# Retrieval scores: the mean's place among the splits, an earlier chunk load, and the groups in which three gathered sums are turned

## The chip, the cores and the metric

One core of one Trainium2 chip runs the whole kernel in one launch. The metric is the device time of a launch in microseconds (us). TensorE (PE), VectorE (DVE), ScalarE (ACT), GpSimd (POOL) and the issue queue of SyncE (SP) run their own instruction streams and meet only at semaphores.

## The reference

Sizes: B = 512 rows, K = 50 indices for each, a table of V = 12500 items of H = 512 numbers, all float32.

```python
retrieved = jnp.mean(item_embeddings[indices], axis=1)
fused_input = jnp.concatenate([user_rep, retrieved], axis=1)
fused_rep = fused_input @ W_fuse + b_fuse
logits = fused_rep @ W_proj + b_proj
```

Many indices lie beyond the table and stand for its last row, so the rows to be fetched are fewer than 50 for each output row.

## The kernel before

**Tiles, chunks, groups.** The 512 rows are four tiles of 128. The 12500 columns of the output are 25 chunks of 500. A group is one tile times one chunk: 12 matmuls of 500 columns, since each product is taken in three parts (the weights and the fused rows are both split into a rounded part, `w_hi` and `f_hi`, and a remainder, `w_lo` and `f_lo`). The groups of tile 0 have one matmul more, for the bias. Chunks 0 to 7 stay in SBUF ("resident"): the kernel runs tile 0 over its eight groups, then tiles 1, 2 and 3. Chunks 8 to 24 are then streamed, each for all four tiles.

**A chunk of weights.** SP loads it in two halves into `w_raw` (two chunks deep, L186); ACT writes `w_hi` (`split_hi`, L316, one instruction a half), DVE writes `w_lo` (`split_lo`, L478, likewise). The load of chunk c waits until the `w_lo` of chunk c - 2 is written. Tile 0's group c waits for both `w_lo` halves of chunk c.

**The gathered sum of a tile.** DVE first sorts the tile's indices (`sort`), so that those inside the table come first. POOL then issues 17 gathers of one row for each partition (L256), each into one slot of a ring of nine, plus gathers into `home` for what is beyond (one, and a second after the copy of L285). A gather waits until the one nine before it has been summed. Columns past a row's last index are skipped inside the gather, so the late gathers of a tile move little. In tile 0, DVE sums the first nine slots and TensorE the other eight and `home` (L582), which leaves the sum turned in a PSUM bank. In tiles 1 to 3 DVE sums all 17 (`add`, L450, `add_pair` for two), `add_last` (L464) and `add_home` (L473); the seventeenth add writes `total`, and TensorE turns it with four transposes (`turn_sum`, L590).

**From the sum to the groups.** ACT scales the turned sum into `ret_t` (`mean`, L328); TensorE multiplies it with the second half of W_fuse (`fuse`, L599, 32 matmuls); ACT writes `f_hi` (`fused_hi`, L333), DVE `f_lo` (`fused_lo`, L491). Tile t + 1 is turned in the middle of tile t's seventh group (c = 6) and fused right behind that group, for all t.

**Banks and stores.** The resident groups and the turned sums of tiles 1 to 3 take three PSUM banks in turn, so each waits for the evacuation of the one three places before. ACT evacuates tile 0's groups (`evacuate_first`, L340), DVE all others (`evacuate`, L506, adds the bias). `out_sb` has three slots; an evacuation waits for the store three groups before it.

**Order on SP ahead of the groups.** After the first loads: wait for tile 0's slot 16, the last of its gathers, then loads of chunks 2 to 5, then for c = 0 and 1 the load of chunk c + 6, a row of the bias, the store of tile 0's group c, and so on. ACT's order there is `split_hi(2)`, `split_hi(3)`, `mean(0)`, `fused_hi(0)`; DVE's is `bias_lo`, `sort(3)`, `add_last(1)`, adds 0 and 1 of tile 1, `split_lo(2)`, adds 2 and 3, `split_lo(3)`, add 4, `fused_lo(0)`.

Of the kernel before, what the change touches and what calls it, by code (L numbers as in the profile page):

```python
# [23 lines left out]
LAPS_AT = 12  # L24
DVE_FIRST = 9
PE_FIRST = PASSING - DVE_FIRST
AHEAD = 5
TURN_EVERY = RESIDENT + 1
HOME_AFTER = 14
OUT_SLOTS = 3  # L30
BIAS_SLOTS = 8
# [3 lines left out]
def retrieval_scores(nc, user_t_in, indices, table, w_fuse, b_fuse, last_item, w_proj, b_proj, out):  # L35
# [4 lines left out]
    LAST = V - 1  # L40
    COLUMNS = SORTED + K
    assert B == TILES * P and H == HK * P and V % CHUNK == 0 and (CHUNKS - 1) % RESIDENT == 0
    assert BASE < SORTED < K and AHEAD + 2 * (RESIDENT - 2) == PASSING
# [7 lines left out]
    with ExitStack() as ctx:  # L51
# [102 lines left out]
        def place(t, i):  # L154
            return (PASSING * t + i) % RING
# [4 lines left out]
        def adds_done(t, i):  # L160
            return (DVE_FIRST + PASSING * (t - 1) if t else 0) + i + 1

        def turn_bank(t):
            return wide_ps[(TURN_EVERY * t - 2) % 3] if t else first_ps

        def group_bank(t, c):
            return wide_ps[(TURN_EVERY * t + c + (c == RESIDENT - 1 and t + 1 < TILES)) % 3]

        def group_of(t, c):
            return TILES * c + t if c >= RESIDENT else RESIDENT * t + c  # L170
# [9 lines left out]
        @block.sync  # L180
        def _(sp):
            def load_chunk(c):
                for h in range(2):
                    if c >= 2:
                        sp.wait_ge(lo_ready, 2 * (c - 2) + h + 1)
                    sp.dma_start(w_raw[:, c % 2, 2 * h:2 * h + 2, :],  # L186
                                 wp_dram[:, 2 * h:2 * h + 2, c * CHUNK:(c + 1) * CHUNK])\
                      .then_inc(w_landed[c % 2][h], 16)

            def load_bias(c):  # L190
                sp.dma_start(bias[:, c % BIAS_SLOTS:c % BIAS_SLOTS + 1, 0:CHUNK],
                             bp_dram[:, c * CHUNK:(c + 1) * CHUNK].unsqueeze(1).to_broadcast([P, 1, CHUNK]))\
                  .then_inc(bias_landed[c % BIAS_SLOTS], 16)

            def store(t, c):
                g = group_of(t, c)
                wait_evacuated(sp, g)
                sp.dma_start(out_dram[t, :, c * CHUNK:(c + 1) * CHUNK], out_sb[:, g % OUT_SLOTS, :])\
                  .then_inc(out_stored[g % OUT_SLOTS], 16)

            sp.dma_start(idx[:, 0:K], indices[:, 0:K]).then_inc(first_idx_landed, 16)
            for k in range(HK):
                sp.dma_start(wf_user[:, k, :], wf_dram[0, :, k, :]).then_inc(wf_user_landed[k], 16)
                if k == 0:
                    sp.dma_start(idx[:, K:TILES * K], indices[:, K:TILES * K]).then_inc(idx_landed, 16)
            sp.dma_start(last_rows[:], last_item.to_broadcast([P, H])).then_inc(last_landed, 16)
            load_chunk(0)
            sp.dma_start(bf_col[:], b_fuse).then_inc(bf_landed, 16)
            load_chunk(1)
            sp.dma_start(wf_ret[:], wf_dram[1]).then_inc(wf_ret_landed, 16)  # L210
            sp.wait_ge(user_fused, 1)
            for row in (0, LO_ROW):
                sp.dma_start(bias_rows[row:row + RESIDENT, :],
                             b_proj[0:RESIDENT * CHUNK].rearrange("(c n) -> c n", n=CHUNK))\
                  .then_inc(bias_rows_landed, 16)
            sp.wait_ge(slot_landed[place(0, PASSING - 1)], 16 * slot_uses(0, PASSING - 1))
            for c in range(2, 6):
                load_chunk(c)
            for c in range(RESIDENT):
                if c < 2:  # L220
                    load_chunk(c + 6)
                if c < RESIDENT - 1:
                    load_bias(c)
                store(0, c)
            load_bias(RESIDENT - 1)
            for c in range(RESIDENT):
                store(1, c)
                if c < 2:
                    load_chunk(RESIDENT + c)
            for c in range(RESIDENT):  # L230
                store(2, c)
            for c in range(RESIDENT):
                store(3, c)
                load_bias(RESIDENT + c)
                if c in (3, 5):
                    load_chunk(RESIDENT + 2 + c // 4)
            for c in range(RESIDENT, CHUNKS):
                for t in range(TILES):
                    store(t, c)
                if c + BIAS_SLOTS < CHUNKS:  # L240
# [65 lines left out]
        def _(act):  # L306
# [45 lines left out]
            act.wait_ge(bias_rows_landed, 32)  # L352
            nc.scalar.copy(bias_split, bias_rows).then_inc(bias_hi_ready, 1)
            split_hi(2)
            split_hi(3)
            mean(0)
            act.wait_ge(bf_landed, 16)
            fused_hi(0)
            for c in range(RESIDENT):
                if c < 2:  # L360
                    split_hi(c + 4)
                if c == RESIDENT - 2:
                    mean(1)
                if c == RESIDENT - 1:
# [11 lines left out]
        def _(dve):  # L376
# [156 lines left out]
            dve.wait_ge(laps_ready, 1)  # L533
            add_home(0)
            bias_lo()
            sort(3)
            add_last(1)
            add_pair(1, 0)
            split_lo(2)
            add_pair(1, 2)  # L540
            split_lo(3)
            add(1, 4)
            fused_lo(0)
            for t in range(TILES):
                for c in range(RESIDENT):
                    if t + 1 < TILES and c < RESIDENT - 2:
                        add_pair(t + 1, AHEAD + 2 * c)
                        if AHEAD + 2 * c + 1 == HOME_AFTER:
                            add_home(t + 1)
                    if t == 0 and c < 4:  # L550
                        split_lo(c + 4)
                    if t + 2 < TILES and c >= RESIDENT - 2:
                        if c == RESIDENT - 2:
                            add_last(t + 2)
                        add_pair(t + 2, 2 * (c - RESIDENT + 2))
                    if t == TILES - 1 and 2 <= c < 6:
                        split_lo(RESIDENT + c // 2 - 1, (c % 2,))
                    if c == RESIDENT - 1 and t + 1 < TILES:
                        fused_lo(t + 1)
                    if t:  # L560
                        evacuate(t, c)
                if t + 2 < TILES:
                    add(t + 2, 4)
            for c in range(RESIDENT, CHUNKS):
                for t in range(TILES):
                    evacuate(t, c)
# [4 lines left out]
        def _(pe):  # L571
# [13 lines left out]

            def turn_sum(t):
                pe.wait_ge(added, adds_done(t, PASSING - 1))
                wait_evacuated(pe, group_of(t - 1, RESIDENT - 4))
# [27 lines left out]
            def project_resident(t, c, halfway=None):  # L616
                g = group_of(t, c)
                if t == 0:
                    pe.wait_ge(lo_ready, 2 * (c + 1))
                if c == RESIDENT - 1 and t + 1 < TILES or t and c == 0:  # L620
                    wait_evacuated(pe, g - 2)
                elif g >= 3:
                    wait_evacuated(pe, g - 3)
# [34 lines left out]
            fuse(0)  # L658
            for t in range(TILES):
                for c in range(RESIDENT):  # L660
                    halfway = t + 1 if c == RESIDENT - 2 and t + 1 < TILES else None
                    project_resident(t, c, halfway)
                    if halfway is not None:
                        fuse(halfway)
# [41 lines left out]
```

## Time and profile before

| what | value |
|---|---|
| runs | 348.36, 352.34, 346.40 us; median 348.36 |
| profiled execution | 348.81 us, of which the span is 347.0 |
| TensorE busy | 322.1 us (93% of the span) |
| DVE, POOL, ACT busy | 183.1, 83.4, 67.5 us |
| granted TensorE clock, mean | 0.97 |
| HBM | 55.47 MB read, 25.60 MB written |

The profile is of one execution. "Idle before" is the time an engine stood still ahead of an instruction; what ended it is inferred from semaphores. Starts are given from the beginning of the span, and 1.8 us of the execution lie outside it.

### The profile page before, as it was taken

What the parts mean: (1) busy time and instruction counts of PE and PEld (TensorE: products, weight loads), DVE (VectorE), ACT (ScalarE), POOL (GpSimd) and SP (SyncE); (2) the same over time, 40 slices, a digit from 0 to 9 for tenths busy, and PEclk for the clock granted to TensorE, in tenths of its full rate; (3) what the DMA queues carried; (4) which work ended last, traced back from release to release, by engine and by line L of the source; (5) the groups of instructions that cost most, each with busy time, mean ns of one, the idle gap of its engine ahead of it and who ended that gap; (6) DMA issues with size and microseconds to landing.
All of it is one profiled execution on the core that took longest, in us unless ns stands there. A gap on an engine that the chain in (4) does not pass through costs nothing.

```text
span 347.0 us, 4203 instructions
## 1 busy us (share of the span) xinstructions
PE 322.1 (93%) x1462; PEld 263.9 (76%) x1462; DVE 183.1 (53%) x294; ACT 67.5 (19%) x102; POOL 83.4 (24%) x87
## 2 busy tenths in 40 slices
PE   4987269969999999999999999999999999999996
PEld 2447268859888888888888888888888888888884
DVE  5698459784667872453454344543445434454222
ACT  2320326522002002403122022220222220220000
POOL 4777777657675700000000000000000000000000
PEclk9998769978999999999999999999999999999999
DMA  7992997996897521589478766787667665452222
GB/s 265 375 361 50 373 401 193 361 379 187 236 389 258 146 107 41 151 225 353 141 226 241 200 165 234 223 240 198 170 231 226 209 228 170 149 188 91 112 94 89
DMA packets 40238, 75.24 MB, mean 217 GB/s; under 512 B 5686, under 2 KB 34630, under 8 KB 40224
## 3 DMA queue, kind: packets, MB, share of 16 engines
q1 hardware_dynamic: 33312, 60.11, 53.1%
q0 software_dynamic: 6336, 13.92, 12.2%
q10 hardware_dynamic: 576, 1.05, 0.8%
q8 instruction: 6, 0.10, 0.1%
q14 instruction: 8, 0.07, 0.1%
HBM read 55.47 MB, written 25.60 MB: 234 GB/s over the span
## 4 chain that ended last, share of the span: by engine, by line
PE 79%; DMA 8%; issue 4%; DVE 4%; POOL 3%; ACT 1%; SPq 0%; POOLq 0%; DVEq 0%; ACTq 0%
PE bank L612 73%; DMA w_raw<-w_proj 5%; PE bank L599 5%; POOL ring L256 3%; DMA ring<-item_embeddings,rows 2%; DVE bank L450 2%; DMA out_sb<-indices 1%; DVE w_lo L478 1%; ACT w_hi L316 1%; PE bank L590 1%; SPq L186 0%; DVE f_lo L491 0%; DVE total L450 0%; DVE bank L473 0%; DVE out_sb L506 0%
## 5 line engine op out<-in xcount | busy, mean ns | idle before, releaser
L612 PE MATMUL bank<-w_hi,f_hi 128*128 (+1 forms) x400 | 156.5, 391 | 0.0
L612 PE MATMUL bank<-w_lo,f_hi 128*128 (+1 forms) x400 | 155.8, 389 | 0.0
L612 PE MATMUL bank<-w_hi,f_lo 128*128 (+1 forms) x400 | 155.5, 389 | 0.0
L506 DVE TENSOR_TENSOR out_sb<-bank,early 128x500 f32<-128x500 f32 x92 | 62.4, 678 | 130.5 <-PE bank L612 125.8
L612 PEld LDWEIGHTS bank<-w_hi,f_lo 128*128 128x128 f32 x400 | 75.4, 188 | 15.6
L612 PEld LDWEIGHTS bank<-w_hi,f_hi 128*128 128x128 f32 x400 | 75.5, 189 | 15.5 <-DVE f_lo L491 0.3
L612 PEld LDWEIGHTS bank<-w_lo,f_hi 128*128 128x128 f32 x400 | 75.5, 189 | 15.0
L316 ACT CAST w_hi<-w_raw 128x1000 fp32r<-128x1000 f32 x50 | 51.0, 1030 | 164.3 <-DMA w_raw<-w_proj 145.9
L256 POOL DMA_INDIRECT ring<-item_embeddings,rows x68 | 70.6, 1038 | 32.0 <-issue 18.2
L478 DVE TENSOR_TENSOR w_lo<-w_raw,w_hi 128x1000 fp32r<-128x1000 f32 x50 | 59.2, 1194 | 2.4 <-ACT w_hi L316 2.4
L450 DVE SCALAR_TENSOR_TENSOR bank<-ring,mask,bank 128x512 f32<-128x512 f32 x56 | 42.3, 755 | 9.7 <-DMA ring<-item_embeddings,rows 6.9
L599 PE MATMUL bank<-ret_t,wf_ret 128*128 128x128 f32 x128 | 17.8, 306 | 9.9 <-ACT ret_t L328 9.9
L599 PEld LDWEIGHTS bank<-ret_t,wf_ret 128*128 128x128 f32 x128 | 17.8, 223 | 10.4 <-issue 10.1
L576 PE MATMUL bank<-early 128*128 128x512 f32 x32 | 16.3, 667 | 4.9 <-DMA early<-w_fuse 4.9
L576 PEld LDWEIGHTS bank<-early 128*128 128x128 f32 x32 | 6.7, 216 | 13.0 <-issue 13.0
L328 ACT ACTIVATE ret_t<-bank 128x128 f32<-128x128 f32 x16 | 3.1, 281 | 41.7 <-PE bank L590 41.7
L491 DVE SCALAR_TENSOR_TENSOR f_lo<-bank,bf_col,f_hi 128x128 fp32r<-128x128 f32 x16 | 4.5, 345 | 10.2 <-ACT f_hi L333 10.2
L582 PE MATMUL bank<-ret_t,ring 128*128 128x128 f32 x32 | 5.4, 322 | 3.8 <-DMA ring<-item_embeddings,rows 3.7
L256 POOL DMA_INDIRECT home<-item_embeddings,lap_row x4 | 7.4, 1844 | 3.6 <-POOL lap_row L285 2.5
L582 PEld LDWEIGHTS bank<-ret_t,ring 128*128 128x128 f32 x32 | 4.7, 225 | 4.3 <-issue 4.3
L333 ACT ACTIVATE f_hi<-bank,bf_col 128x128 fp32r<-128x128 f32 x16 | 4.6, 369 | 14.9 <-PE bank L599 14.9
L340 ACT COPY out_sb<-bank 128x500 f32<-128x500 f32 x8 | 4.6, 576 | 10.4 <-PE bank L612 7.9
(58 smaller groups left out, 55.1 us busy)
## 6 DMA issues: line engine op xcount, KB each, us to landing
w_raw<-w_proj SPq DMA_DIRECT2D x50, 500.0 KB, 6.6
logits<-out_sb SPq DMA_DIRECT2D x100, 250.0 KB, 2.4
early<-b_proj SPq DMA_DIRECT2D x25, 250.0 KB, 5.2
ring<-item_embeddings,rows POOLq DMA_INDIRECT x68, 5.8
early<-user_t ACTq DMA_DIRECT2D x4, 256.0 KB, 4.4
early<-w_fuse SPq DMA_DIRECT2D x4, 256.0 KB, 6.0
wf_ret<-w_fuse SPq DMA_DIRECT2D x1, 1024.0 KB, 18.5
last_rows<-last_item SPq DMA_DIRECT2D x1, 256.0 KB, 7.0
```

The lines of the kernel that those rows point to most:

```text
L256: return nc.gpsimd.indirect_dma_start(out=to, out_offset=None, in_=table, in_offset=bass.IndirectOffsetOnAxis(ap=column, axis=0), **how)
L316: nc.scalar.copy(w_hi[:, slot, 2 * h:2 * h + 2, :], w_raw[:, c % 2, 2 * h:2 * h + 2, :])\
L333: nc.scalar.activation(f_hi[:, t, n, :], fused_ps[n][:, t * P:(t + 1) * P], ACT.Identity, bias=bf_col[:, n:n + 1]).then_inc(f_hi_ready, 1)
L340: nc.scalar.copy(out_sb[:, c % OUT_SLOTS, :], group_bank(0, c)[:, 0:CHUNK]).then_inc(first_evacuated, 1)
L450: nc.vector.scalar_tensor_tensor(total[:] if i == PASSING - 1 else total_ps[:], here, mask[:, t, i + 1:i + 2], total_ps[:], ALU.mult, ALU. ...
L478: nc.vector.tensor_tensor(w_lo[:, c % RESIDENT, 2 * h:2 * h + 2, :], w_raw[:, c % 2, 2 * h:2 * h + 2, :], w_hi[:, c % RESIDENT, 2 * h:2 * ...
L491: nc.vector.scalar_tensor_tensor(f_lo[:, t, n, :], fused_ps[n][:, t * P:(t + 1) * P], bf_col[:, n:n + 1], f_hi[:, t, n, :].bitcast(F32), A ...
L506: nc.vector.tensor_tensor(out_sb[:, g % OUT_SLOTS, :], ps[:, 0:CHUNK], bias[:, c % BIAS_SLOTS, 0:CHUNK], ALU.add).then_inc(evacuated, 1)
L576: m = nc.tensor.matmul(fused_ps[n][:, :], wf_user[:, k, n * P:(n + 1) * P], user_t[:, k, :], start=(k == 0), stop=(k == HK - 1))
L582: m = nc.tensor.matmul(first_ps[:, k * P:(k + 1) * P], rows_in[:, k * P:(k + 1) * P], taken, start=(first and k == 0), stop=last, skip_gro ...
L599: m = nc.tensor.matmul(fused_ps[n][:, t * P:(t + 1) * P], wf_ret[:, k, n * P:(n + 1) * P], ret_t[:, k, :], start=False, stop=(k == HK - 1) ...
L612: m = nc.tensor.matmul(ps[:, 0:CHUNK].unsqueeze(1), f[:, t, k, :], w, start=begin, stop=(f is f_lo and k == HK - 1))
```

## The change

ACT takes `mean(0)` between `split_hi(2)` and `split_hi(3)`. SP loads chunk 2 behind a wait for slot 12 of tile 0, and chunks 3 to 5 behind the old wait for slot 16. DVE does `split_lo(2)` ahead of `sort(3)`, and has its adds of tile 1 placed later, behind `split_lo(3)` and `fused_lo(0)`, still five of them ahead of the loop. A table, `TURN_AT = (6, 5, 5)`, says in which group of tile t the next tile is turned: tile 1 still in the seventh, tiles 2 and 3 now in the sixth. The adds of a tile are dealt out to the groups by that table, `split_lo(7)` moves from the fourth group of tile 0 to its seventh, and the order of the banks is read from a list (`bank_order`) with its waits (`bank_freed`).

```diff
-AHEAD = 5
-TURN_EVERY = RESIDENT + 1
+TURN_AT = (6, 5, 5)
...
+        bank_order = []
+        for t in range(TILES):
+            for c in range(RESIDENT):
+                bank_order.append((t, c))
+                if t + 1 < TILES and c == TURN_AT[t]:
+                    bank_order.append((t + 1, "turn"))
+
         def turn_bank(t):
-            return wide_ps[(TURN_EVERY * t - 2) % 3] if t else first_ps
+            return wide_ps[bank_order.index((t, "turn")) % 3] if t else first_ps
...
+        def bank_freed(engine, t, c):
+            place_before = bank_order.index((t, c)) - 3
+            if place_before >= 0 and bank_order[place_before][1] != "turn":
+                wait_evacuated(engine, group_of(*bank_order[place_before]))
...
+            sp.wait_ge(slot_landed[place(0, LAPS_AT)], 16 * slot_uses(0, LAPS_AT))
+            load_chunk(2)
             sp.wait_ge(slot_landed[place(0, PASSING - 1)], 16 * slot_uses(0, PASSING - 1))
-            for c in range(2, 6):
+            for c in range(3, 6):
                 load_chunk(c)
...
             split_hi(2)
+            mean(0)
             split_hi(3)
-            mean(0)
             act.wait_ge(bf_landed, 16)
             fused_hi(0)
...
             bias_lo()
+            split_lo(2)
             sort(3)
             add_last(1)
-            add_pair(1, 0)
-            split_lo(2)
-            add_pair(1, 2)
+            add(1, 0)
             split_lo(3)
-            add(1, 4)
+            add(1, 1)
             fused_lo(0)
+            add(1, 2)
+            add_pair(1, 3)
             for t in range(TILES):
+                turn_at = TURN_AT[t] if t + 1 < TILES else RESIDENT
+                ahead = PASSING - 2 * turn_at
                 for c in range(RESIDENT):
-                    if t + 1 < TILES and c < RESIDENT - 2:
-                        add_pair(t + 1, AHEAD + 2 * c)
-                        if AHEAD + 2 * c + 1 == HOME_AFTER:
+                    if c == RESIDENT - 1 and t + 1 < TILES:
+                        fused_lo(t + 1)
+                    if t + 1 < TILES and c < turn_at:
+                        add_pair(t + 1, ahead + 2 * c)
+                        if ahead + 2 * c + 1 == HOME_AFTER:
                             add_home(t + 1)
-                    if t == 0 and c < 4:
-                        split_lo(c + 4)
-                    if t + 2 < TILES and c >= RESIDENT - 2:
-                        if c == RESIDENT - 2:
+                    if t == 0 and c in (0, 1, 2, RESIDENT - 2):
+                        split_lo(min(c + 4, RESIDENT - 1))
+                    if t + 2 < TILES and c >= turn_at:
+                        if c == turn_at:
                             add_last(t + 2)
-                        add_pair(t + 2, 2 * (c - RESIDENT + 2))
+                        add_pair(t + 2, 2 * (c - turn_at))
...
-                if t + 2 < TILES:
-                    add(t + 2, 4)
+                for i in range(2 * (RESIDENT - turn_at), PASSING - 2 * TURN_AT[t + 1] if t + 2 < TILES else 0):
+                    add(t + 2, i)
...
                 for c in range(RESIDENT):
-                    halfway = t + 1 if c == RESIDENT - 2 and t + 1 < TILES else None
+                    halfway = t + 1 if t + 1 < TILES and c == TURN_AT[t] else None
                     project_resident(t, c, halfway)
```

## Rows read from the trace of the kernel before

**Rows 1.** TensorE's idle times: waiting line, releaser, us in total, times, longest

```profile
PE bank L599 <- ACT ret_t L328: 9.9, 1, 9.9
PE bank L590 <- DVE total L450: 3.2, 1, 3.2
```

**Rows 2.** The chain that ended last: start us, us, what

```profile
46.66 4.74 PE bank L599 x26
...
74.72 1.11 PE bank L590 x4
...
78.34 4.76 PE bank L599 x32
...
103.72 0.44 PE bank L590 x4
...
105.51 3.57 PE bank L599 x32
```

**Rows 3.** Timeline of ACT: start us, us, instructions [idle before]

```profile
45.31 1.02 ACT L316 CAST w_hi<-w_raw 128x1000 fp32r<-128x1000 f32 x1 [1.86 <-DMA w_raw<-w_proj]
46.24 0.77 ACT L328 ACTIVATE ret_t<-bank 128x128 f32<-128x128 f32 x4
```

**Rows 4.** POOL's gathers for tile 0 (12, 16), tile 1 (16), tile 2 (16)

```profile
25.92 1.34 POOL L256 DMA_INDIRECT ring<-item_embeddings,rows  x1 [0.30 <-issue]
...
31.48 0.99 POOL L256 DMA_INDIRECT ring<-item_embeddings,rows  x1 [0.30 <-issue]
...
58.26 0.99 POOL L256 DMA_INDIRECT ring<-item_embeddings,rows  x1 [0.39 <-issue]
...
91.16 1.01 POOL L256 DMA_INDIRECT ring<-item_embeddings,rows  x1 [1.24 <-DVE bank L450]
```

**Rows 5.** DMA issues one by one, us to landing: gathers at 25.92, 31.48, 58.26

```profile
ring<-item_embeddings,rows POOLq DMA_INDIRECT x1, 3.5
ring<-item_embeddings,rows POOLq DMA_INDIRECT x1, 2.1
ring<-item_embeddings,rows POOLq DMA_INDIRECT x1, 6.3
```

**Rows 6.** The same of SP: chunk 2's halves (33.59, 34.03), a store at 61.6

```profile
w_raw<-w_proj SPq DMA_DIRECT2D x1, 500.0 KB, 4.2
w_raw<-w_proj SPq DMA_DIRECT2D x1, 500.0 KB, 5.7
logits<-out_sb SPq DMA_DIRECT2D x1, 250.0 KB, 8.2
```

**Rows 7.** Timeline of TensorE: the last sum of tile 0

```profile
35.68 1.06 PE L582 MATMUL bank<-out_sb,ring 128*128 128x128 f32 x8
```

**Rows 8.** Timeline of DVE: sort(3) begins, add_last(1), fused_lo(0), loop, totals of tiles 1, 2

```profile
31.48 0.21 DVE L394 MAX8 key_sorted<-out_sb 128x8 f32<-128x50 f32 x1
...
33.70 0.76 DVE L464 TENSOR_SCALAR bank<-last_rows,n_left 128x512 f32<-128x512 f32 x1 [0.20 <-DVE rows L406]
...
51.88 1.13 DVE L491 SCALAR_TENSOR_TENSOR f_lo<-bank,bf_col,f_hi 128x128 fp32r<-128x128 f32 x4 [3.64 <-ACT f_hi L333]
52.92 1.61 DVE L450 SCALAR_TENSOR_TENSOR bank<-ring,mask,bank 128x512 f32<-128x512 f32 x2
...
56.73 1.60 DVE L450 SCALAR_TENSOR_TENSOR bank<-ring,mask,bank 128x512 f32<-128x512 f32 x2
...
73.92 0.75 DVE L450 SCALAR_TENSOR_TENSOR total<-ring,mask,bank 128x512 f32<-128x512 f32 x1
...
101.31 0.75 DVE L450 SCALAR_TENSOR_TENSOR total<-ring,mask,bank 128x512 f32<-128x512 f32 x1
```

**Rows 9.** Stretches: PE busy, PEld, DVE, ACT, POOL, granted clock, DMA share, GB/s

```profile
30.00:34.00 4.00, 4.00 (x25) 4.00 (x25) 3.47 (x15) 0.00 (x0) 2.99 (x3) 0.64 0.05 8
64.00:70.00 6.00, 6.00 (x28) 5.00 (x27) 4.35 (x5) 2.79 (x4) 2.84 (x3) 1.00 1.03 398
76.00:83.00 7.00, 7.00 (x39) 6.53 (x38) 2.72 (x5) 1.77 (x8) 5.07 (x6) 0.66 0.85 278
```

More of the change, by code:

```diff
@@ L42, in retrieval_scores @@
     assert B == TILES * P and H == HK * P and V % CHUNK == 0 and (CHUNKS - 1) % RESIDENT == 0
-    assert BASE < SORTED < K and AHEAD + 2 * (RESIDENT - 2) == PASSING
+    assert BASE < SORTED < K and HOME_AFTER % 2 == 0
     user_dram = user_t_in.rearrange("(k p) n -> k p n", p=P)
@@ L161, in adds_done @@
             return (DVE_FIRST + PASSING * (t - 1) if t else 0) + i + 1
+        bank_order = []
[4 more added lines that the diff above has]
+                    bank_order.append((t + 1, "turn"))
         def turn_bank(t):
-            return wide_ps[(TURN_EVERY * t - 2) % 3] if t else first_ps
+            return wide_ps[bank_order.index((t, "turn")) % 3] if t else first_ps
         def group_bank(t, c):
-            return wide_ps[(TURN_EVERY * t + c + (c == RESIDENT - 1 and t + 1 < TILES)) % 3]
+            return wide_ps[bank_order.index((t, c)) % 3]
+        def bank_freed(engine, t, c):
+            place_before = bank_order.index((t, c)) - 3
+            if place_before >= 0 and bank_order[place_before][1] != "turn":
+                wait_evacuated(engine, group_of(*bank_order[place_before]))
         def group_of(t, c):
@@ L361, in _ @@
                     split_hi(c + 4)
-                if c == RESIDENT - 2:
+                if c == TURN_AT[0]:
                     mean(1)
-                if c == RESIDENT - 1:
+                if c == TURN_AT[0] + 1:
                     fused_hi(1)
@@ L535, in _ @@
             bias_lo()
+            split_lo(2)
             sort(3)
             add_last(1)
-            add_pair(1, 0)
-            split_lo(2)
-            add_pair(1, 2)
+            add(1, 0)
             split_lo(3)
-            add(1, 4)
+            add(1, 1)
             fused_lo(0)
+            add(1, 2)
+            add_pair(1, 3)
             for t in range(TILES):
+                turn_at = TURN_AT[t] if t + 1 < TILES else RESIDENT
+                ahead = PASSING - 2 * turn_at
                 for c in range(RESIDENT):
-                    if t + 1 < TILES and c < RESIDENT - 2:
-                        add_pair(t + 1, AHEAD + 2 * c)
-                        if AHEAD + 2 * c + 1 == HOME_AFTER:
+                    if c == RESIDENT - 1 and t + 1 < TILES:
[3 more added lines that the diff above has]
+                        if ahead + 2 * c + 1 == HOME_AFTER:
                             add_home(t + 1)
-                    if t == 0 and c < 4:
-                        split_lo(c + 4)
-                    if t + 2 < TILES and c >= RESIDENT - 2:
-                        if c == RESIDENT - 2:
+                    if t == 0 and c in (0, 1, 2, RESIDENT - 2):
+                        split_lo(min(c + 4, RESIDENT - 1))
+                    if t + 2 < TILES and c >= turn_at:
+                        if c == turn_at:
                             add_last(t + 2)
-                        add_pair(t + 2, 2 * (c - RESIDENT + 2))
+                        add_pair(t + 2, 2 * (c - turn_at))
                     if t == TILES - 1 and 2 <= c < 6:
                         split_lo(RESIDENT + c // 2 - 1, (c % 2,))
-                    if c == RESIDENT - 1 and t + 1 < TILES:
-                        fused_lo(t + 1)
                     if t:
                         evacuate(t, c)
-                if t + 2 < TILES:
-                    add(t + 2, 4)
+                for i in range(2 * (RESIDENT - turn_at), PASSING - 2 * TURN_AT[t + 1] if t + 2 < TILES else 0):
+                    add(t + 2, i)
             for c in range(RESIDENT, CHUNKS):
@@ L587, in turn_sum @@
                 pe.wait_ge(added, adds_done(t, PASSING - 1))
-                wait_evacuated(pe, group_of(t - 1, RESIDENT - 4))
+                bank_freed(pe, t, "turn")
                 for k in range(HK):
@@ L619, in project_resident @@
                     pe.wait_ge(lo_ready, 2 * (c + 1))
[L620 to L623, printed above, removed]
+                bank_freed(pe, t, c)
                 if g == 0:
```

## The prediction

> **What bounds the kernel now.** I read TensorE's idle times first, since it is busy 93% of the span. From its first group to the end it waits once: 3.2 us for the finished sum of tile 1. Before that it waits 9.9 us for ACT's `ret_t` [rows 1]. Everything behind is matmul, so the question is how much earlier the two waits end, and whether new ones open. The chain of waits puts the first wait's end at 46.66 and the turn of tile 1 at 74.72 [rows 2].
>
> The first wait is one of order. TensorE finished tile 0's last sum at 35.68 + 1.06 = 36.74 [rows 7], but ACT took the mean at 46.24, behind the second half of chunk 3's split, which began at 45.31 when its load landed [rows 3]. That load stood behind chunk 2's, which SP issued only at 31.48 + 2.1 = 33.6, when slot 16 had landed [rows 4 to 6]. Just before, from 30 to 34 us, the DMA engines stood almost still, at 8 GB/s [rows 9].
>
> **The change, step by step.** Starts are of the profiled execution (348.81 us; the median of the runs is 348.36, so the same sum stands 0.4 lower there).
>
> *Chunk 2's load.* Slot 12's gather was issued at 25.92 and landed 3.5 later, at 29.4 [rows 4, 5]. So the load goes out 4.2 us earlier. With the landings of before (4.2 and 5.7 us, taken beside tile 1's gathers, so an upper bound) the halves are there at 33.7 and 35.6 [rows 6], and ACT's splits (1.02 each [rows 3]) end by 36.7, just as TensorE ends its sum. SP's later loads wait for slot 16 as before; nothing but they is queued behind the new wait.
>
> *The mean.* At 36.8 to 37.5 instead of 46.24. TensorE then fuses at about 37.3, without having stood still long, at full clock: 3.6 us as at 105.51, against 4.8 at 46.66 [rows 2]. It is done at 40.9. But `f_hi` and `f_lo` do not follow at once: ACT now has chunk 3's split ahead of `fused_hi(0)`, and DVE has `split_lo(3)` and an add ahead of `fused_lo(0)`. That is where the stall goes.
>
> *fused_lo(0), called F.* Low bound, by DVE's own queue: `w_lo` of chunk 2 done 36.3 if its load lands a little faster on the idle engines; sort(3) 33.70 - 31.48 = 2.2; then three of 0.8 (add_last, two adds) and 2.3 for `split_lo(3)` [rows 8]: F = 43.2, and 44.8 with the landings above. By the loads: if slot 16 lands as before at 33.6, chunk 3 takes the place that chunk 2 had, lands by 39.7, and sets nothing. High bound: slot 16's gather, now beside chunk 2's load, takes the 6.3 us of the last gather of tile 1 [rows 5] and lands at 37.8; chunk 3 then lands at 43.9 and F is 43.9 + 1.0 + 1.2 + 0.8 = 46.9. I take 44.3, between the first two, since that gather moves almost nothing and chunk 2 is mostly in by 34.5. Before, F was 51.88 [rows 8]: 7.6 us earlier.
>
> *Up to the turn of tile 1.* Four things must be there.
> TensorE itself: before it needed 71.56 - 51.88 = 19.7 us from F to the middle of group 6 [rows 2, 8]; that gives 64.0, and since it idled 3.4 us ahead of F, as long as the idle time after which the granted clock was 0.66 [rows 1, 9], I add 1 to 3 us at half speed: 65 to 67.
> DVE: 1.0 for `fused_lo`, 2.5 for three adds, three steps of a pair and a split at 56.73 - 52.92 = 3.8, then 5.7 for three pairs and `home`: F + 20.6 = 64.9 [rows 8]. Moving `split_lo(7)` behind this takes 2.3 us and a wait for chunk 7 out of it; before, from F to the total's end was 22.8.
> Gathers: POOL issues one each 1.3 us, waiting for nothing that the change moves, so the last of tile 1 stays at 58.26; landing as before, 6.3 later, and the add: 65.4 [rows 4, 5].
> The bank: it waits for group 4's evacuation, which waits for group 1's store, which SP issues behind chunk 7's load, so behind `split_lo(5)` at F + 11.1 = 55.4 and 1 us of issues; with 8.2 us to land [rows 6] and the copy, 65.2.
> Three floors lie together at 65, and the DMA engines, full at 400 GB/s in this stretch [rows 9], have to move in it much that they moved later before. I take 66.7 for the turn, 1.5 above the floors, against 74.72: 8.0 us gained. TensorE comes at 65 to 67, so it waits under 2 us.
>
> *Clock at the turn.* Before, turn, half a group and fuse took from 74.72 to 83.10, 8.4 us, with a granted clock of 0.66 on the mean of 76 to 83; the same for tile 2, at full clock, took from 103.72 to 109.08, 5.4 us [rows 2, 9]. Without the 3.2 us wait 3.0 us are gained.
> The Trainium skill's page "TensorE: Matmul & The Clock Gate", section "Part 1: The HAM clock gate", says that the array falls to half clock when it idles and comes back only under sustained work. By that rule, which the trace bears out here, the gain at the turn hangs on the rest of the wait being short, and the wait ahead of group 0 costs more than its length.
>
> *Turns of tiles 2 and 3.* No work is added. Each turn comes one group earlier: from 83.10 to 103.72 TensorE did one group of tile 0 and 6.5 of tile 1, so 2.7 us for one [rows 2]. POOL's last gather for tile 2 stood at 91.16, after waits for DVE [rows 4]; with DVE earlier POOL can run without them, as from 31.48 to 58.26, 26.8 us for a tile: 85.1, landed (2.1 to 6.3) by 87.2 to 91.4 [rows 4, 5]. DVE has seven adds ahead of tile 1's groups now, not five. I put the total at about 89, from DVE's steps of one pair and one evacuation, and TensorE's arrival at 66.7 + 5.4 + one group of 2.9 + 5.5 of 2.7 = 89.9. Tight, cost 0 to 3, taken 0.5. Tile 3 follows after eight groups, turn and fuse, some 26 us of TensorE against POOL's 26.8: within that term. The bank list changes no wait that ends last.
>
> Sum: -8.0 - 3.0 + 0.5 = -10.5; 348.8 - 10.5 = 338.3 us.
>
> **The rivals.**
> *The wait at the turn stays long.* Total or bank come at 68 to 70, TensorE at 65, the clock falls as before: the 3.0 are not gained, and the turn gives 5 to 7. Time 342 to 344. For it: full DMA engines, three floors within half a microsecond. Against: a late F delays TensorE too.
> *Chunk 2's load holds up tile 0's last gathers.* F = 46.9, total 67.5 and up; TensorE at 68 to 69.5; turn at 69: -5.7 - 3.0 + 0.5, 340.6 us. For it: 6.3 us for a near-empty gather under load. Against: few bytes, 2.1 us alone [rows 5].
> The Trainium skill's page "DMA: Bandwidth & Descriptors", section "Queues, rings and completion order", has each DMA engine take turns between its queues, a packet at a time. By that rule the gathers do share with the load, and this rival would be the likelier; no row of before has these two side by side at that place.
> *The change does little.* The DMA engines, not the order, set the pace: six chunks of 1.02 MB, 19 gathers of up to 0.26 and some eight bias rows and stores of 0.26 are up to 13.2 MB, which at the 0.4 MB a us of the full engines [rows 9] takes 33 us; counted from 31.4 that is 64.4, and with stores queued behind loads the turn could slip to 71 or more. Time 345 to 349. Against: the late gathers skip most of their rows, and the stores that the turn needs are the first two only.
> *Slower.* Tile 2's total does not come earlier, since POOL keeps waiting for slots: it stays at 101.31 + 0.75 = 102.1 [rows 8]. Then the turn is at 102.1, not 103.72, but with one group more behind it: -1.6 + 2.7 + 3.0 of clock = +4.1, 352.9 us. It decides where the total comes later than 98. Against: its waits for DVE came from adds that are now 8 us earlier.
> *Better.* Everything lands at the floors, turn at 64.5: 335.5.
>
> **How the numbers follow.** Forecast (336.5 to 341) 0.42, the held-up gathers (340 to 341.4) 0.15, better 0.08, long wait 0.22, little gained 0.09, slower 0.04. Within 2% of the median, about what a measurement of this kernel can tell from no change, is 341.4 to 355.3. Faster by over 2%: 0.42 + 0.15 + 0.08 and a little of the long wait, 0.67; within: 0.31; slower by over 2% would need the slower case at two turns: 0.02. The range runs from below the better case to the long wait: 334 to 344.5; it leaves out the two last cases and a bit.
>
> **What would show it.** The mean near 37 and TensorE's wait for `ret_t` under 1 us; a new wait of 3 to 5 us for `f_lo`; the turn of tile 1 near 66.7 and its three parts in 5.4 us; waits under 1.5 us at the turns of tiles 2 and 3. I am wrong if slot 16 lands after 37.8, if the turn of tile 1 comes after 69, or if a later turn waits over 3 us.

## The result, and the profile after

The changed kernel took 345.47 us (median of 20 runs, 343.08 to 348.19), the kernel before in the same comparison 347.90. The ratio is 0.9916, with an interval of 0.9887 to 0.9944: 2.4 us between the medians, 0.8% by the ratio, where 10.5 us had been forecast. It is a gain, but a small one, and the time lies 1 us above the predicted range of 334 to 344.5. A ratio compares the means of the executions in a chip's faster state, while a time here is the median of all executions, so the quotient of two times need not equal the ratio.

TensorE's waits in the profile after (who waited, for whom: us in total, times, longest), which answer to [rows 1]:

```profile
PE bank L606 <- DVE total L463: 6.8, 2, 3.7
PE bank L592 <- DMA early<-w_fuse: 5.5, 1, 5.5
PE bank L598 <- DMA ring<-item_embeddings,rows: 4.2, 4, 2.9
PE bank L628 <- DVE f_lo L504: 2.4, 1, 2.4
PE bank L615 <- ACT ret_t L341: 0.5, 1, 0.5
```

The 9.9 us for `ret_t` are down to 0.5, as meant. In their place stand 2.4 for `f_lo` and 6.8, in two waits, for a finished sum: 3.2 before, at one turn.

TensorE's timeline after (start, us, what, and in brackets the idle time ahead and what ended it):

```profile
39.08 3.81 PE L615 MATMUL bank<-ret_t,wf_ret 128*128 128x128 f32 x32 [0.46 <-ACT ret_t L341]
45.52 0.49 PE L628 MATMUL bank<-w_hi,f_hi 128*128 128x500 f32 x1 [2.41 <-DVE f_lo L504]
...
68.53 0.85 PE L606 MATMUL bank<-ident,total 128*128 128x128 f32 x4 [3.71 <-DVE total L463]
71.68 4.02 PE L615 MATMUL bank<-ret_t,wf_ret 128*128 128x128 f32 x32
...
96.70 1.12 PE bank L606 x4
97.82 2.22 PE bank L628 x6
100.04 3.57 PE bank L615 x32
103.61 20.39 PE bank L628 x90
124.00 0.44 PE bank L606 x4
```

(The last five lines are of the chain of waits: start, us, what; they answer to [rows 2].) The mean, `F` (the start of `fused_lo(0)`) and the turn of tile 1 came 7.6, 6.8 and 6.2 us earlier than before. The turn of tile 1 then took 75.70 - 68.53 = 7.2 us with its half group and fuse, against 8.4, so 7.4 us were gained by then. At the turn of tile 2, 3.10 us of waiting and 103.61 - 96.70 = 6.9 us, where 5.4 had been enough, take 4.6 of these back. The last matmul ends at 341.04, before at 343.84: 2.8 us.

DVE around the turn of tile 2, after the change, same columns:

```profile
87.11 0.76 DVE L463 SCALAR_TENSOR_TENSOR bank<-ring,mask,bank 128x512 f32<-128x512 f32 x1 [1.35 <-DMA ring<-item_embeddings,rows]
87.77 0.67 DVE L519 TENSOR_TENSOR out_sb<-bank,early 128x500 f32<-128x500 f32 x1
91.52 0.76 DVE L463 SCALAR_TENSOR_TENSOR bank<-ring,mask,bank 128x512 f32<-128x512 f32 x1 [3.08 <-DMA ring<-item_embeddings,rows]
92.99 0.76 DVE L463 SCALAR_TENSOR_TENSOR bank<-ring,mask,bank 128x512 f32<-128x512 f32 x1 [0.71 <-DMA ring<-item_embeddings,rows]
...
95.90 0.75 DVE L463 SCALAR_TENSOR_TENSOR total<-ring,mask,bank 128x512 f32<-128x512 f32 x1
```

DVE is no longer behind its work but behind the gathers: 5.1 us of idle time in front of gathers 12, 13 and 14 of tile 2. (The diff of the change also moves `fused_lo(t + 1)` ahead of the adds of the eighth group, which its description leaves out. DVE then idled 2.39 us ahead of it, at 75.47, with adds undone; that did not set this turn, since DVE had caught up and stood waiting when gather 12 landed.) The issue of gather 13 of tile 2, its landing (last number, us), and the landing of gather 12 of tile 1:

```profile
83.75 1.00 POOL L269 DMA_INDIRECT ring<-item_embeddings,rows  x1 [0.30 <-DVE bank L463]
...
ring<-item_embeddings,rows POOLq DMA_INDIRECT x1, 7.7
...
ring<-item_embeddings,rows POOLq DMA_INDIRECT x1, 9.1
```

The first landing belongs to the issue at 83.75, the second to that of gather 12 of tile 1 at 54.33. SP's loads of chunks 8 and 9 are issued at 83.39 and 85.52. From 83 to 90 us the windows (PE, PEld, DVE, ACT, POOL busy, granted clock, DMA share, GB/s) of before and then of after read:

```profile
83.00:90.00 7.00, 7.00 (x33) 5.80 (x33) 4.35 (x9) 1.18 (x4) 5.59 (x5) 1.00 0.57 133
```

```profile
83.00:90.00 7.00, 7.00 (x32) 5.82 (x31) 3.99 (x6) 0.00 (x0) 5.45 (x6) 1.00 1.01 291
```

### The profile page after: what moved, and what is told of

It reads as the page before. It is cut to its first block, busy times and chain, and to the rows that moved or that the text cites. A ratio compares the mean times of both kernels' runs of the same rounds, so it can differ in the third digit from the quotient of the medians.

```text
span 344.2 us, 4202 instructions
## 1 busy us (share of the span) xinstructions
PE 321.6 (93%) x1462; PEld 262.3 (76%) x1462; DVE 182.7 (53%) x294; ACT 67.8 (20%) x102; POOL 84.8 (25%) x87
## 4 chain that ended last, share of the span: by engine, by line
PE 71%; DVE 0%; issue 0%
PE bank L628 68%; PE bank L615 2%; PE bank L606 0%; DVE total L463 0%; DVE out_sb L519 0%
## 5 line engine op out<-in xcount | busy, mean ns | idle before, releaser
L592 PE MATMUL bank<-early 128*128 128x512 f32 x32 | 16.9, 689 | 5.5 <-DMA early<-w_fuse 5.5
L615 PEld LDWEIGHTS bank<-ret_t,wf_ret 128*128 128x128 f32 x128 | 15.3, 196 | 0.9 <-issue 0.6
L615 PE MATMUL bank<-ret_t,wf_ret 128*128 128x128 f32 x128 | 15.3, 279 | 0.5 <-ACT ret_t L341 0.5
L606 PE MATMUL bank<-ident,total 128*128 128x128 f32 x12 | 2.6, 351 | 6.8 <-DVE total L463 6.8
L598 PE MATMUL bank<-ret_t,ring 128*128 128x128 f32 x32 | 4.3, 282 | 3.6 <-DMA ring<-item_embeddings,rows 3.6
L606 PEld LDWEIGHTS bank<-ident,total 128*128 128x128 f32 x12 | 1.7, 169 | 7.8 <-DVE total L463 7.7
L598 PEld LDWEIGHTS bank<-ret_t,ring 128*128 128x128 f32 x32 | 3.8, 191 | 3.9 <-issue 3.9
```

Source lines behind the costliest of these rows:

```text
L592: m = nc.tensor.matmul(fused_ps[n][:, :], wf_user[:, k, n * P:(n + 1) * P], user_t[:, k, :], start=(k == 0), stop=(k == HK - 1))
L598: m = nc.tensor.matmul(first_ps[:, k * P:(k + 1) * P], rows_in[:, k * P:(k + 1) * P], taken, start=(first and k == 0), stop=last, skip_gro ...
L615: m = nc.tensor.matmul(fused_ps[n][:, t * P:(t + 1) * P], wf_ret[:, k, n * P:(n + 1) * P], ret_t[:, k, :], start=False, stop=(k == HK - 1) ...
```

## The experiments

Chips differed. Those called **kind one** run the kernel before in about 348 us; those of **kind two** in 351 to 353, and there every variant, the changed kernel too, was slower than before. Times are compared on one chip only, and across chips only by the ratio to the kernel before on the same chip. In the expectations, "the slower kind" is kind two. An expectation may name its theories by a letter. A is that the turns in the sixth group cost what is missing. B is that the loads of chunks 8 and 9 make those gathers late. P is that the full DMA engines, not `F`, set the turn of tile 1.

Edits, short (all against the changed kernel):

```diff
 # SEVENTH
-TURN_AT = (6, 5, 5)
+TURN_AT = (6, 6, 6)
 # LOADS LATE: chunks 8 and 9 behind tile 2's stores
                 store(1, c)
-                if c < 2:
-                    load_chunk(RESIDENT + c)
             for c in range(RESIDENT):
                 store(2, c)
+                if c < 2:
+                    load_chunk(RESIDENT + c)
 # BIAS LATE: tile 0's loop on SP
-                if c < RESIDENT - 1:
-                    load_bias(c)
+                if c >= 4:
+                    for b in range(2 * (c - 4), min(2 * (c - 4) + 2, RESIDENT - 1)):
+                        load_bias(b)
 # LOAD BACK: chunk 2 behind slot 16 again
-            sp.wait_ge(slot_landed[place(0, LAPS_AT)], 16 * slot_uses(0, LAPS_AT))
-            load_chunk(2)
...
-            for c in range(3, 6):
+            for c in range(2, 6):
 # MEAN BACK
-            mean(0)
             split_hi(3)
+            mean(0)
```

DVE BACK is DVE's old order ahead of the loop with `split_lo(c + 4)` for c < 4.

### Chips of kind one

**changed_3**, the changed kernel itself, and **turns_seventh_3**, SEVENTH, on one chip.

> The changed kernel beside before on a further chip. Two readings stand against each other: 0.9916 where before runs in 347.9 us, and 1.0129 where before runs in 352.7. If the sign goes with the chip's state (there, engines took up to 3 us longer to go on after something that had long been done), then a before of about 348 us comes with 0.99 and one of about 353 with 1.01.

> The changed kernel with the turns of tiles 2 and 3 in the seventh group, beside it. So far 1.0207 and 1.0098 to before on two chips of the slower kind, where the changed kernel has 1.0129: no gain shown. Theory A: on a chip with before at 348 us it is 3 to 4.6 us faster than the changed kernel (ratio 0.977 to 0.983) and the wait at the turn of tile 2 is gone; on one with before at 353 it is within 2 us of it, since late stores and late f_hi set the turns there. Theory B: within 1.5 us of the changed kernel on either.

Measured: 346.05 against 347.91 us (0.9936, 0.9903 to 0.9969), and 341.76 (0.9838, 0.9787 to 0.9889). The chains, of changed_3:

```profile
95.09 0.76 DVE total L463
...
95.89 1.11 PE bank L606 x4
97.01 2.25 PE bank L628 x6
99.26 3.57 PE bank L615 x32
...
128.61 211.68 PE bank L628 x936
```

and of turns_seventh_3:

```profile
96.15 0.76 DVE total L463
...
96.96 0.66 PE bank L606 x4
97.61 1.35 PE bank L628 x6
98.97 3.57 PE bank L615 x32
...
128.30 208.98 PE bank L628 x924
```

With the earlier turn the total comes only 1.1 us forward, and 1.0 of that was there at the turn of tile 1 (66.61 against 67.61), before the two programs differ in their turns. TensorE, which arrives a group earlier, waits 3.52 us instead of 1.57 and loses full clock, so both fuses end at nearly the same time (102.83, 102.54). Then the sixth-group version has one group more behind it: x936 against x924, 2.7 us. With the 0.3 that is 3.0 us in the profiles; the medians differ by 4.3. The intervals do not meet: the turns in the sixth group cost, and do not gain.

**loads89_late_2**, LOADS LATE with the turns as in the change, **seventh_loads_late**, SEVENTH with LOADS LATE, **seventh_bias_late_2**, SEVENTH with BIAS LATE, and **best**, all three; on one chip, before 347.50.

> The changed kernel (turns of tiles 2 and 3 in the sixth group) with the loads of chunks 8 and 9 behind the first stores of tile 2. In the trace of the changed kernel tile 2's gathers issued at 83.7 to 87.7 us landed 6.3 to 7.9 us later and DVE stood 5.1 us for them. Theory B (the 2 MB of chunks 8 and 9 hold them up): they land in 3 to 5 us, DVE's idle time falls to 1 or 2, the total comes 3 us earlier, and the wait of 3.1 us and the 1.5 us at half clock go: ratio to before about 0.980 where the changed kernel has 0.9925. Theory A (no room for the turn): total within 1 us, ratio 0.989 to 0.994.

> Both: turns of tiles 2 and 3 in the seventh group and the loads of chunks 8 and 9 later. With the turn in the seventh group alone a wait of 1.6 us was left at the turn of tile 2 (total at 96.9) and the ratio was 0.984. Theory B: this wait goes too, ratio near 0.979, within 0.3% of loads89_late_2, since the place of the turn does not matter once the total is early. Theory A: no change against 0.984.

> Turns in the seventh group and the bias rows of chunks 0 to 6 later (two ahead of each store of tile 0 from the fifth on). If the full DMA engines at 52 to 66 us set the turn of tile 1: chunk 6's second half and the gathers 12 to 16 of tile 1 land 1 to 2 us sooner, the wait of 3.8 us there falls to under 2.5, the clock stays up, 2 to 3.5 us less than with the turns in the seventh group alone: ratio 0.974 to 0.979. If DVE's chain from fused_lo(0) on sets it: 0.983 to 0.985.

> All three: turns in the seventh group, bias rows late, loads of chunks 8 and 9 late. If both collisions are real, their gains add: ratio 0.970 to 0.976, near 338 us, with waits under 1 us at the turn of tile 2 and under 2.5 us at that of tile 1. If only one is, 0.978 to 0.980.

| kernel | us | ratio (interval) | F | wait and turn of tile 1 | wait and turn of tile 2 |
|---|---|---|---|---|---|
| changed_3 (other chip) | 346.05 | 0.9936 (0.9903 to 0.9969) | 43.03 | 3.90, 66.61 | 3.52, 95.89 |
| turns_seventh_3 (other chip) | 341.76 | 0.9838 (0.9787 to 0.9889) | 44.08 | 3.83, 67.61 | 1.57, 96.96 |
| loads89_late_2 | 344.36 | 0.9930 (0.9893 to 0.9966) | 42.63 | 3.43, 65.75 | 2.16, 93.00 |
| seventh_loads_late | 341.08 | 0.9825 (0.9792 to 0.9859) | 44.95 | 1.15, 67.33 | none, 93.79 |
| seventh_bias_late_2 | 340.86 | 0.9818 (0.9781 to 0.9856) | 42.83 | 4.13, 66.64 | none, 95.38 |
| best | 341.40 | 0.9842 (0.9801 to 0.9882) | 43.6 | 1.87, 66.77 | none, 92.81 |

Moving the loads away does empty the stretch of the turn of tile 2; the same window in loads89_late_2:

```profile
83.00:90.00 7.00, 7.00 (x32) 5.80 (x31) 2.75 (x4) 0.00 (x0) 5.17 (x7) 1.00 0.43 106
```

and the total of tile 2 starts at 92.20, not 95.09 (0.9 of this was there at the turn of tile 1). The profiled execution of loads89_late_2 is shorter too, 342.61 against 345.26, but on another chip, and the ratios of the two kernels agree within their intervals. Its DVE:

```profile
86.77 0.75 DVE L463 SCALAR_TENSOR_TENSOR bank<-ring,mask,bank 128x512 f32<-128x512 f32 x1 [3.78 <-DMA ring<-item_embeddings,rows]
...
92.20 0.75 DVE L463 SCALAR_TENSOR_TENSOR total<-ring,mask,bank 128x512 f32<-128x512 f32 x1
```

Gather 12 was issued at 80.76 and landed 6.0 us later even so, and from there DVE has 6.2 us of its own (five adds, home and two evacuations), whatever the later gathers do. So A holds, and B only in part: without the loads gathers 13 and 14 took 5.4 and 4.3 us to land, with them 7.7 and 7.9 in the first profile of the changed kernel, but the chain behind gather 12 stays. A second pair on one chip says the same as the first: with the loads late in both, the turns in the seventh group take 341.08 us and those in the sixth 344.36, and their intervals do not meet. With the turns in the seventh group the four variants agree within their intervals, so neither later loads nor later bias rows add anything measurable. In the two profiles with LOADS LATE and SEVENTH the wait that went at tile 2 came up at tile 3. DVE's longest wait of best between 100 and 125 us:

```profile
DVE bank L464 <- DMA ring<-item_embeddings,rows: 5.5, 1, 5.5
```

TensorE waited 2.93 us there for tile 3's total, and 1.73 in seventh_loads_late. BIAS LATE was to shorten the wait at the turn of tile 1; at 4.13 us in one profile and 1.87 in the other it can't be told, since the kernels without it, which on kind one are the same program up to that turn, show 1.15 to 3.90. The 1.15 is no earlier total either: TensorE came late, at 66.18, having lost full clock in its first groups.

### Chips of kind two

What each part of the change is worth alone was to be told by the following, and was not, since they fell on such chips.

**turns_seventh**, **loads89_late**, **turns_only** (LOAD BACK, MEAN BACK, DVE BACK: the new turns alone) and **load_back**, on one chip, before 352.82.

> The changed kernel with tiles 2 and 3 turned in the seventh group again (all else of the change kept). Theory A, that the turn in the sixth group is what took the gain back: TensorE comes to the turn of tile 2 one group later, near 96.3 us, when the total is done (95 to 96.7), so the 3.1 us wait and the 1.5 us at half clock behind it go: 4.6 us less than the changed kernel, near 340.8 us, ratio to before about 0.978. Theory B, that the late gathers of tile 2 are held up by the loads of chunks 8 and 9 whatever the turn: the total comes later too, a wait of 1 to 3 us stays, and the time is within 2 us of the changed kernel. Theory C, that the early part brought little: ratio near 0.99 in any case.

> The changed kernel with the loads of chunks 8 and 9 behind the first two stores of tile 2 instead of those of tile 1; turns of tiles 2 and 3 stay in the sixth group. Theory B, that these 2 MB at 83 to 87 us hold up tile 2's last gathers (landing 7.7 us behind issue): without them the gathers land some 3 us after issue, DVE's idle times of 1.4, 3.1 and 0.7 us go, the total is done near 92, and the wait at the turn of tile 2 goes: 4 to 4.6 us less than the changed kernel, near 341. Theory A, that there is no room for a turn in the sixth group (POOL's issue or DVE's seven adds): the total comes at 95 or later still, and the time stays within 1.5 us of the changed kernel.

> The kernel before with only the turns of tiles 2 and 3 in the sixth group (the loads, the place of the mean and DVE's order ahead of the first group as before). By theory A TensorE comes to the turn of tile 2 at 101.0 us, one group earlier than before; the total was done at 102.1 and now depends on DVE having seven adds ahead of tile 1 instead of five: 0 to 1.5 us of wait there, so 0 to 3 us slower than before. If the sixth group costs by itself, whatever the state of the early part, it is 3 to 6 us slower; if the cost comes from the collision of an earlier TensorE with gathers that did not get earlier, it is within 1.5 us of before.

> The changed kernel with chunk 2's load behind slot 16 again. Slot 16's gather lands 2.1 us after its issue, not 3.6, so the load is issued near 34, and DVE's first split of chunk 2 is ready near 39 instead of 35; F (the first remainder of the fused rows) comes 3 to 4 us later, near 48.5. If the turn of tile 1 is set by what follows F on DVE, it comes 1.5 to 3.5 us later (the 2 us wait for chunk 6 and the 0.7 us for a gather shrink) and tile 2's turn loses part of its 3.1 us wait: time 0 to 2 us over the changed kernel. If the DMA engines set the turn of tile 1, no difference beyond 1 us.

Measured: 360.19 (1.0207, 1.0154 to 1.0260), 359.94 (1.0194, 1.0146 to 1.0242), 358.80 (1.0162, 1.0111 to 1.0211), 359.58 (1.0173, 1.0120 to 1.0226). No theory had all four slower. Their executions also scatter more: the six of turns_seventh took 354.08 to 362.37 us, on kind one 340.23 to 345.20.

**changed_again**, **turns_seventh_2**, **seventh_bias_late** and **before_again**, the last being the kernel before, on a second chip, before 352.72.

> The changed kernel as it is, beside the kernel before on one chip. If the times of the chip of the first four kernels (before 352.8 us there, 347.9 elsewhere) hold for this one too, the ratio to before could be above 1: there TensorE stood still for up to 4.5 us ahead of a matmul with nothing in the profile that released it, and on a chip or in a build where that happens the changed kernel should show it too (theory D, ratio 1.01 to 1.02). If that belonged to the edits, the ratio is 0.99 as before and TensorE has no such wait (theory A).

> The same kernel as turns_seventh, now beside the changed kernel on one chip. Theory A: 3 to 4.6 us less than the changed kernel, no wait at the turn of tile 2. Theory B: within 1.5 us of it, with a wait of 1 to 3 us there. If the unexplained standstill of TensorE returns, its length is to be taken off both.

> As turns_seventh, and the seven bias rows of chunks 0 to 6 (0.26 MB each) are loaded from the fifth store of tile 0 on, two ahead of each store, not one ahead of each of the first seven. They are needed only from tile 1's first evacuation on. If the full DMA engines between 52 and 66 us set the turn of tile 1 (a near-empty gather took 9.1 us there, chunk 6's second half 7.3), chunk 6 and the gather land 1 to 2 us sooner, the 3.7 us wait at that turn falls to 1 to 2 us, and with it its stretch at half clock: 1.5 to 3.5 us less than turns_seventh. If DVE's chain sets it, no more than 0.5 us.

> The kernel before with a profile on the same chip. If it shows waits of TensorE that nothing releases, these belong to the chip; if it has none there, and the others do, they belong to the kernels.

Measured: 358.58 (1.0129, 1.0067 to 1.0190), 356.55 (1.0098, 1.0056 to 1.0140), 359.15 (1.0173, 1.0118 to 1.0227), and one execution at 353.82. The changed kernel is one program with 0.9916 and 0.9936 on kind one and 1.0129 here, so the sign goes with the chip or with its state at that time, which these runs can't part. The changed kernel and turns_seventh_2 lie within each other's intervals here. TensorE's waits in changed_again, then in turns_seventh_2:

```profile
PE bank L628 <- issue: 6.5, 6, 2.1
...
PE bank L606 <- issue: 5.0, 1, 5.0
```

```profile
PE bank L615 <- ACT ret_t L341: 12.0, 2, 8.7
```

"issue" is a standstill with no cause in the records. It falls on other places from run to run, mostly at `ret_t` or a turn. The kernel before, in before_again, has none of this kind on TensorE, which by the expectation would lay them on the changed kernels. But the changed kernel has none on kind one, and in before_again ACT and DVE have waits that before does not show:

```profile
ACT f_hi L333 <- remote: 12.9, 2, 7.1
...
DVE f_lo L491 <- issue: 7.2, 2, 3.8
```

"remote" stands for another core or an unknown queue. So neither the chip nor the program explains them alone. All profiles of kind two also lack the landing times of most transfers, as of these loads in before_again (in before the same line ends in 6.6 us), so what their waits are put down to is less sure:

```profile
w_raw<-w_proj SPq DMA_DIRECT2D x50, 500.0 KB
```

**mean_only** (before with the mean moved; like the changed kernel it has `fused_lo(t + 1)` ahead of the adds of the eighth group), **turns_only_2**, **seventh_load_back** and **seventh_mean_back**, on a third chip, before 351.09.

> The kernel before with only the mean of tile 0 ahead of chunk 3's split. The mean comes near 40.8 instead of 46.2; fused_lo(0) waits for DVE's split of chunk 3 and an add, near 48.3 instead of 51.9. The turn of tile 1 waits for chunk 7's split as before; by theory F it comes 3.6 us earlier, ratio 0.989 to 0.991. By the kernel's old order it could be that loads behind split_lo(5) hold it: then 1 to 2 us, 0.994 to 0.997.

> The kernel before with only the turns of tiles 2 and 3 in the sixth group, on a chip of the first kind. TensorE comes to the turn of tile 2 at 101.0 us, the total is done near 100 to 102: wait of 0 to 1.5 us, ratio 1.000 to 1.005. If the sixth group costs by itself, as in the changed kernel (4.3 us): 1.010 to 1.014.

> Turns in the seventh group, chunk 2's load behind slot 16 again. fused_lo(0) then starts near 47.5 instead of 44, TensorE comes to the middle of group 6 near 67 instead of 64. Theory P (POOL's gathers, the last issued near 60 us and landed 6 later, set the turn of tile 1): the turn stays at 67 to 68.5, the wait falls from 3.8 to under 1.5 us, the clock stays at full speed behind it, and the time is that of the kernel with the load in place: ratio 0.981 to 0.986. Theory F (the turn follows fused_lo(0)): turn near 70.5 to 71, 3 us slower, ratio 0.991 to 0.993.

> Turns in the seventh group, the mean of tile 0 behind the split of chunk 3 again (early load and DVE's order kept). The mean then comes near 42.5 instead of 38.5, fused_lo(0) near 47 instead of 44, since TensorE fuses from 43 on. Theory P: turn of tile 1 at 67 to 68.5 with a wait under 1.5 us, ratio 0.981 to 0.986. Theory F: 3 us slower, 0.991 to 0.993.

Measured: 357.88 (1.0184, 1.0143 to 1.0225), 356.89 (1.0192, 1.0142 to 1.0242), 356.21 (1.0114, 1.0052 to 1.0176), 361.51 (1.0226, 1.0154 to 1.0297). ACT in mean_only:

```profile
39.87 1.02 ACT L327 CAST w_hi<-w_raw 128x1000 fp32r<-128x1000 f32 x1 [0.79 <-DMA w_raw<-w_proj]
46.12 0.78 ACT L339 ACTIVATE ret_t<-bank 128x128 f32<-128x128 f32 x4 [5.22 <-remote]
```

The split that is ahead of the mean ended at 40.89, TensorE's sum at 35.78, and yet ACT went on only at 46.12. This engine waited 5.2 us for something long done, and the order of the work does not explain it.

## Why the prediction was wrong

Right were the first steps. The mean was taken at 38.66 (36.8 forecast) and F was 45.12 (44.3). Of either delay 0.7 us was there before the change could act: gather 12 of tile 0 was issued at 26.61, not 25.92. Beside chunk 2's load (207 GB/s from 30 to 34 us, where there were 8 [rows 9]) the gather of slot 16 landed after 3.6 us, not 2.1 [rows 5], and TensorE ended its last sum at 38.62, not 36.74. The Trainium skill's page "DMA: Bandwidth & Descriptors", section "Queues, rings and completion order", lets each DMA engine alternate between its queues; the later landing agrees with it. That the load is the whole cause is not shown: load_back, with the load back in its old place, ended that sum at 39.22, on a chip of kind two. From F to the middle of group 6 TensorE took 64.82 - 45.12 = 19.7 us, as forecast. The 1 to 3 us for a fallen clock ahead of group 0 did not come: the wait was 2.41 us, not 3 to 5, and the clock stayed at 1.00.

What came then at tile 1 matches the rival "the wait at the turn stays long", which had 0.22 and 342 to 344 us: total at 68.48, TensorE at 64.82, the clock fallen. With tile 2 on top the time lies beyond it. Of the signs named, a later turn did wait over 3 us (3.10). Three terms failed; together they are the missing 7.7 us.

- **Turn of tile 1, -8.0: measured -6.2 (miss 1.8).** 0.8 of it is F. The rest is that DVE idled 2.0 us for chunk 6's second half (load issued at 52.5, landed 7.3 later) and 0.7 for gather 12 of tile 1, issued at 54.33 and landed after 9.1. DVE's own work from F was right: 20.6 us forecast, and 20.6 + 2.0 + 0.7 = 23.3 of the 23.4 measured to the turn. I had costed the floors one by one and added 1.5 for full engines; the waits inside DVE's own queue were no floor of mine, and they are the ones that came last.
- **Clock at the turn, -3.0: measured -1.2 (miss 1.8).** I had TensorE wait "under 2 us", by adding the cold start that did not occur to its arrival. It came at 64.82 and waited 3.71, and the clock fell again: 0.79 from 68 to 76. With a wait of 1.15 it stayed up, as the windows from 68 to 76 us of turns_seventh_3 (wait 3.83) and of seventh_loads_late (1.15) show:

```profile
68.00:76.00 8.00, 8.00 (x48) 7.26 (x47) 5.45 (x10) 2.51 (x9) 6.34 (x6) 0.79 1.00 357
```

```profile
68.00:76.00 8.00, 7.86 (x51) 6.81 (x51) 6.37 (x12) 2.99 (x10) 6.22 (x6) 1.00 1.04 406
```

The length of the wait alone does not decide it. A wait of 2.16 us at tile 2 in loads89_late_2 was followed by a fallen clock, one of 2.93 at tile 3 in best was not:

```profile
93.00:101.00 8.00, 8.00 (x47) 7.48 (x48) 4.70 (x7) 1.93 (x8) 6.17 (x7) 0.79 0.93 311
```

```profile
122.00:130.00 8.00, 8.00 (x54) 7.33 (x55) 2.34 (x6) 1.93 (x8) 0.00 (x0) 1.00 0.17 65
```

Ahead of group 0 the changed kernel's 2.41 us left the clock up, and 2.56 in seventh_loads_late was followed by 0.79 from 45 to 53. So the cold start that I feared there is real in some executions, and that it stayed away in this one was luck.

- **Turns of tiles 2 and 3, +0.5: measured +4.6 (miss 4.1).** The step that failed is the total "at about 89, from DVE's steps". I had the last gather land by 87.2 to 91.4, and yet let the total follow DVE's steps alone, without going on from each landing to the work of DVE behind it. DVE's steps were no dearer than thought: from the end of tile 1's fuse to the total's end I had 89 - 72.1 = 16.9 us, measured were 21.0, of which 5.1 were waits for gathers 12 to 14. Gather 12 landed at 87.1 with some 6 us of DVE's work in series behind it, so 93 at the earliest; gathers 13 and 14, beside the loads of chunks 8 and 9, which are issued just there, made it 96.65, and TensorE came at 93.60. So in this profile gathers 13 and 14 made the wait; in loads89_late_2, with TensorE there at 90.84 and the total at 92.95, the chain behind gather 12 did. 3.1 us of wait and 1.5 of lost clock followed. POOL kept its pace (27.4 us from tile 1's last gather to tile 2's, 26.8 forecast), but tile 1's last gather, which I had held fixed at 58.26, was issued at 60.29. The rival "slower" had the same outline, the turn that moves forward by less than one group's time, but tied it to POOL's waits for slots; those did shorten.

-10.5 + 1.8 + 1.8 + 4.1 = -2.8, as in the traces.

That the turns in the sixth group cost is shown by experiment, on two chips of kind one: by 4.3 us on the first, where the kernel without them gains 1.6% and the changed kernel 0.6%, and by 3.3 us on the second. They are not the whole shortfall. The first two terms alone promised -11.0 us, and turns_seventh_3 gives -6.2: what is missing there is read from traces (the waits at tile 1, and 1.57 us left at tile 2), and no variant gained more than 1.8%. How the 1.6% divides between the earlier load, the mean's place and DVE's order is open, as those runs fell on chips of kind two. One hint: in all 20 profiles, with F between 42.63 and 52.58, the turn of tile 1 follows F by 20.9 to 23.8 us (F 42.63 with 65.75, F 48.07 with 70.85). For the second of these, seventh_load_back, P had 67 to 68.5 and theory F (the turn follows F) 70.5 to 71. This speaks against P, without settling it, as that run too is of kind two.

## What to carry to other kernels

Moving a step forward in TensorE's order gains only if its operand comes forward by more than the work that now lies behind it; here a turn one group (2.7 us) earlier needed a total 2.7 us earlier and got 1.1 at most. To find when an operand can be there, follow the whole serial tail of the engine that makes it, from each transfer that it waits for, not from the last one alone. When a stall goes, ask at once which transfers now fall together.

## What was not expected of the hardware

- The gather of slot 16, which moves almost nothing, took 2.1 us to land where the DMA engines were idle, 6.3 beside full ones [rows 5], and 3.6 beside chunk 2's load. Gathers 12 of tile 1 and 13 of tile 2 in the changed kernel, which come earlier in their tiles and so move more (no row shows the first to be near-empty, as an expectation calls it), took 9.1 and 7.7, with the engines at a share of 0.95 from 54 to 64 us and 1.01 from 83 to 90.
- In the changed kernel, waits of TensorE of 3.71 and 3.10 us were each followed by a clock of 0.79 over eight microseconds, and one of 2.41 left it at 1.00. In the variants 2.16 and 2.56 were followed by 0.79, and 1.15, 1.57 and 2.93 by 1.00. The Trainium skill's page "TensorE: Matmul & The Clock Gate", section "Part 1: The HAM clock gate", ties the fall to idleness; the longer waits agree, and the mixed outcomes from 2.16 to 2.93 show that the length of a single wait does not tell it. What else does is open.
- Chips differ by 0.9 to 1.5% for the kernel before, and by 3.6 to 5.4% for the kernels after it that ran on both kinds, with standstills of 3 to 9 us on ACT and TensorE behind work long done. What causes them is open. A gain of 0.6 to 1.8% on one chip was a loss of 1 to 2% on another, so variants are compared on one chip only.
